# A selective-scan decoder layer: B and C in one transfer per scan group

## The reference, cut to what matters

```python
dbc = jnp.einsum('bld,rd->blr', u, W_x)
dt_in = dbc[..., :DTR]                    # DTR = 16
Bm = dbc[..., DTR:DTR + DSTATE]           # DSTATE = 16
Cm = dbc[..., DTR + DSTATE:]
dA = jnp.exp(dt[..., None] * A)
dBu = dt[..., None] * Bm[:, :, None, :] * u[..., None]
def step(h, e):
    da, dbu, c = e
    h = da * h + dbu
    y = jnp.einsum('bdn,bn->bd', h, c)
    return (h, y)
```

## Time and profile before

| what | value |
|---|---|
| median of 3 runs | 1865.69 us (1863.43 to 1866.33) |
| the profiled execution | 1863.23 us, of which the span is 1861.2 us |
| busy: TensorE, VectorE, ScalarE, GpSimd | 73%, 73%, 53%, 48% |
| moved by DMA | 188.89 MB, mean 101 GB/s |
| mean granted clock of TensorE | 0.849 of full speed |

### The profile page before, as it was taken

The page is one execution under the profiler, slowest core; times in us unless marked ns, Lnnn a source line. Parts: engine busy times, 40 slices in busy tenths (PEclk is TensorE's granted clock), DMA queues, the critical chain, the costliest instruction groups (busy, mean ns, idle before and its releaser), DMA issues.

```text
span 1861.2 us, 16320 instructions
## 1 busy us (share of the span) xinstructions
PE 1366.2 (73%) x5472; PEld 826.3 (44%) x5472; DVE 1350.9 (73%) x1509; ACT 987.5 (53%) x1519; POOL 898.0 (48%) x459
## 2 busy tenths in 40 slices
PE   5555767686797758885778667887588857786975
PEld 2344344453455335552456334553355434562433
DVE  3987588957876888867888687867878778773142
ACT  4432665547663655647554655637465566534532
POOL 0665077615764266624666165642667155651110
PEclk9555978897899879998799978998799978998988
DMA  5632343205330532206321343305332153310000
GB/s 182 241 124 79 100 163 118 86 26 214 113 109 27 189 108 102 80 24 204 113 101 56 120 136 114 106 23 183 102 112 79 36 193 112 112 34 0 12 0 23
DMA packets 64762, 188.89 MB, mean 101 GB/s; under 512 B 6224, under 2 KB 22480, under 8 KB 64720
## 3 DMA queue, kind: packets, MB, share of 16 engines
q1 hardware_dynamic: 64720, 188.37, 29.3%
HBM read 183.62 MB, written 4.72 MB: 101 GB/s over the span
## 4 chain that ended last, share of the span: by engine, by line
PE 40%; DVE 31%; ACT 15%; issue 6%; POOL 5%; DMA 2%; ACTq 0%; DVEq 0%; POOLq 0%; SPq 0%; another core or an unknown queue 0%
DVE reg_a L1078 16%; DVE pb L1069 8%; PE py L645 6%; PE pc L631 5%; PE pc L623 4%; PE pb L486 4%; PE pb L605 3%; POOL reg_a L443 3%; ACT reg_a L875 2%; PE px L549 2%; PE px L527 2%; DMA x_out<-reg_m 2%; PE pb L587 2%; ACT xs L778 2%; DVE reg_m L927 1%
## 5 line engine op out<-in xcount | busy, mean ns | idle before, releaser
L443 POOL TENSOR_TENSOR reg_a<-reg_a,cb 128x1024 f32<-128x1024 f32 x256 | 611.7, 2391 | 438.1 <-DVE reg_a L1078 437.8
L1078 DVE TENSOR_TENSOR_SCAN reg_a<-reg_a,pb 128x1024 f32<-128x1024 f32 x256 | 584.6, 2283 | 143.5 <-ACT reg_a L875 110.2
L875 ACT ACTIVATE reg_a<-dt,neg_a 128x511 f32<-128x511 f32 x512 | 335.6, 711 | 165.3 <-DVE reg_a L1078 164.6
L645 PE MATMUL py<-ident,reg_a 128*128 128x128 f32 x2048 | 329.9, 318 | 70.6 <-POOL reg_a L443 70.6
L645 PEld LDWEIGHTS py<-ident,reg_a 128*128 128x128 f32 x2048 | 288.9, 167 | 167.6 <-POOL reg_a L443 104.9
L1069 DVE TENSOR_TENSOR pb<-bb,pb 128x1024 f32<-128x1024 f32 x256 | 314.6, 1229 | 29.7 <-ACT reg_y L835 2.6
L564 PE MATMUL pb<-ex,vw 64*128 64x512 f32 x48 | 46.9, 1075 | 146.9 <-DVE px L994 146.9
L623 PE MATMUL pc<-x2T,w_fc 128*128 128x512 f32 x224 | 119.0, 658 | 28.1 <-DVE reg_y L1095 21.2
L549 PE MATMUL px<-hT,whh 128*128 128x512 f32 x288 | 137.4, 613 | 0.4 <-ACT xs L778 0.4
L631 PE MATMUL pc<-w_pr,reg_m 128*128 128x256 f32 x448 | 109.8, 396 | 7.0 <-ACT y_sb L798 4.1
L405 POOL TENSOR_TENSOR xs<-xs,hT 128x1024 f32<-128x1024 f32 x24 | 56.6, 2358 | 96.2 <-ACT xs L786 96.2
(11 more groups left out here) (174 smaller groups left out, 2259.5 us busy)
## 6 DMA issues: line engine op xcount, KB each, us to landing
bb<-bc_rows SPq DMA_DIRECT2D x256, 512.0 KB, 3.7
cb<-bc_rows SPq DMA_DIRECT2D x64, 512.0 KB, 6.0
xin<-x_in SPq DMA_DIRECT2D x9, 512.0 KB, 3.6
xs<-x_in SPq DMA_DIRECT2D x8, 512.0 KB, 3.6
x_out<-reg_m SPq DMA_DIRECT2D x8, 512.0 KB, 3.4
w_in<-w_inT_in SPq DMA_DIRECT2D x1, 1024.0 KB, 7.1
w_fc<-w_fcT_in SPq DMA_DIRECT2D x1, 1024.0 KB, 10.9
w_pr<-w_prT_in SPq DMA_DIRECT2D x1, 1024.0 KB, 13.1
```

The lines of the kernel that those rows point to most:

```text
L443: pool.tensor_tensor(h[:, g % HR], h[:, g % HR], cb[:, 2 * q:2 * q + 2], ALU.mult).then_inc(s["hc_done"], 1)
L645: mm = pe.matmul(py[:, cols_], h[:, g % HR, j, cols_], ident[:], is_transpose=True, start=(q == 0 and j == 0 and i2 == 0), stop=(q == PAIR ...
L875: ins = act.activation(d_a[:, g % 2, j, 1:], dt[:, c, 1:], ACT.Exp, scale=neg_a[:, c * NS + n + j:c * NS + n + j + 1])
L1078: dve.tensor_tensor_scan(h2[:, g % HR], d_a2[:, g % 2], pb[:, 1:3, :].rearrange("p a t -> p (a t)"), 0.0, ALU.mult, ALU.add).then_inc(s["s ...
```

## The change

B and C of a group come in one transfer of 1 MB. `bc` is a ring of four slots, each with two rows of B and two rows of C. `cb` is gone, so C is loaded again for every chunk: 32 transfers of 1 MB in an iteration in place of 32 + 8 of 512 KB. So that the four rows of a pair lie side by side in DRAM, the columns of `w_x` are put in the order B, B, C, C on the host, and the set-up scales the columns of B in eight pieces. A slot is free again when GpSimd's product with C is done (`hc_done`), not when `mul` is.

```diff
-HB = 3
+HB = 4
...
-        cb = sb("cb", [P, NS, L])
         xp = sb("xp", [P, L])
-        bb = sb("bb", [P, HB, 2, L])
+        bc = sb("bc", [P, HB, 4, L])
...
-        def pair(half, q):
-
-            return bc_dram[half, 2 * q:2 * q + 2, :].rearrange("n t -> (n t)").partition_broadcast(P)
+        def pair(q):
+
+            return bc_dram[4 * q:4 * q + 4, :].rearrange("n t -> (n t)").partition_broadcast(P)
...
                     for half in range(2):
-                        sp_.dma_start(bc_dram[half], xp[Q * half + DTR:Q * (half + 1), :]).then_inc(s["bc_out"], 16)
+                        sp_.dma_start(bc_dram[NS * half:NS * (half + 1), :], xp[Q * half + DTR:Q * (half + 1), :]).then_inc(s["bc_out"], 16)
                     sp_.wait_ge(s["bc_out"], 32)
                     for g in range(GROUPS):
                         q = g % PAIRS
                         if g >= HB:
-                            sp_.wait_ge(s["mul_done"], g - HB + 1)
-                        sp_.dma_start(bb[:, g % HB].rearrange("p n t -> p (n t)"), pair(0, q)).then_inc(s[f"b_in{g % HB}"], 16)
+                            sp_.wait_ge(s["hc_done"], g - HB + 1)
+                        sp_.dma_start(bc[:, g % HB].rearrange("p n t -> p (n t)"), pair(q)).then_inc(s[f"bc_in{g % HB}"], 16)
                         if g == STORE_AT and spikes:
                             store_out(i)
-                        if g < PAIRS:
-                            sp_.dma_start(cb[:, 2 * q:2 * q + 2, :].rearrange("p n t -> p (n t)"), pair(1, q)).then_inc(s[f"cb_in{q}"], 16)
...
                         pool.wait_ge(s["scan_done"], g + 1)
-                        pool.wait_ge(s[f"cb_in{q}"], 16)
-                        pool.tensor_tensor(h[:, g % HR], h[:, g % HR], cb[:, 2 * q:2 * q + 2], ALU.mult).then_inc(s["hc_done"], 1)
+                        pool.wait_ge(s[f"bc_in{g % HB}"], 16 * (g // HB + 1))
+                        pool.tensor_tensor(h[:, g % HR], h[:, g % HR], bc[:, g % HB, 2:4], ALU.mult).then_inc(s["hc_done"], 1)
...
-            dve.tensor_scalar(w_x[:, :, DTR:Q], w_x[:, :, DTR:Q], 0.5, None, ALU.mult)
+            for half in range(2):
+                for q in range(PAIRS // 2):
+                    b_cols = w_x[:, :, Q * half + DTR + 4 * q:Q * half + DTR + 4 * q + 2]
+                    dve.tensor_scalar(b_cols, b_cols, 0.5, None, ALU.mult)
...
-                    dve.wait_ge(s[f"b_in{g % HB}"], 16 * (g // HB + 1))
+                    dve.wait_ge(s[f"bc_in{g % HB}"], 16 * (g // HB + 1))
...
-                    dve.tensor_tensor(pb[:, 1:3, :], bb[:, g % HB], pb[:, 0:1, :].to_broadcast([P, 2, L]),
+                    dve.tensor_tensor(pb[:, 1:3, :], bc[:, g % HB, 0:2], pb[:, 0:1, :].to_broadcast([P, 2, L]),
                                       ALU.mult).then_inc(s["mul_done"], 1)
```

More of the change, by code:

```diff
@@ L85 @@
 z_full zth_ready sz_ready sp_abs sp_exp sp_ln dt_ready dtu_ready da_zero yt_ready yback_full
-bc_kept bc_out cb_in0 cb_in1 cb_in2 cb_in3 cb_in4 cb_in5 cb_in6 cb_in7 b_in0 b_in1 b_in2 da_ready mul_done scan_done hc_done hsum_done ypost_done yz_done
+bc_kept bc_out bc_in0 bc_in1 bc_in2 bc_in3 da_ready mul_done scan_done hc_done hsum_done ypost_done yz_done
 op_half op_full res_done post_stat post_aggr post_ve post_rs post_norm post_full hT_loaded
@@ L1129 @@
     w_x = w["L0_attn_W_x"].T
+    w_bc = w_x[:, DTR:].reshape(DIN, 2, PAIRS, 2).transpose(0, 2, 1, 3).reshape(DIN, BC)
     blank = np.zeros((DIN, Q - DTR), w_x.dtype)
@@ L1137 @@
         "w_inT_in": w["L0_attn_W_in"].T,
-        "w_xT_in": np.concatenate([w_x[:, :DTR], w_x[:, DTR:DTR + NS], w_x[:, :DTR], w_x[:, DTR + NS:],
+        "w_xT_in": np.concatenate([w_x[:, :DTR], w_bc[:, :NS], w_x[:, :DTR], w_bc[:, NS:],
                                    w_x[:, :DTR], blank, w_x[:, :DTR], blank], axis=1),
@@ L1148 @@
     out = nc.dram_tensor("x_out", (BATCH, L, E), F32, kind="ExternalOutput").ap()
-    bc_dram = nc.dram_tensor("bc_rows", (2, NS, L), F32, kind="Internal").ap()
+    bc_dram = nc.dram_tensor("bc_rows", (BC, L), F32, kind="Internal").ap()
     decoder_layer(nc, bc_dram, *args, out)
```

## The result

The changed kernel takes 1878.68 us in the median (1878.44 to 1882.86, 4 runs), against 1864.74 us (1863.43 to 1866.33, 4 runs) for the one before: 1.008 of it, 95% interval [1.0062, 1.0097]. It is 13.9 us slower. The forecast was no change, 1867.2 us.

The account below looks back on a forecast made before the run. TensorE and VectorE bound the kernel, loads being off the path; 1.5 us lost at one head and 0 elsewhere, on the 1865.69 us median, gave 1867.2 us, called no change, range 1861 to 1874.

Parts of the forecast that it names:

- What it adds: Extra loads, later slot release, set-up scalings: seven more cost under 7 x 0.75 = 5 us uncovered, nothing under 11.19 us idle.
- Can the transfers carry it: Densest stretch of groups: 1 MB per 3.7 us needs 283 GB/s; DMA had moved 399 GB/s, so groups would not stretch.
- How late 1 MB lands: Loads into `bc`: complete 5.0 to 5.7 us after issue in the ring, 6.6 us at a batch's head.
- Head of batch 0: First load lands after 6.6 us; scan 2.4 us later, 1.0 us hidden by ScalarE's decay: 1.5 us lost.
- Heads of 1 to 7: First load may land 8.3 us after issue because the scan waits for the decay; 6.6 us fits, nothing lost.
- The ring: Four slots: from product g-4's end to `mul` g at least 7.2 us, median 11.8; landing 5.7 us, so nothing lost.
- The skill's figure: Landing of 1 MB by the skill page: 6.15 us transfer plus about 2.0 fixed, near 8.2; sum 5.6 instead of 1.5 us.
- the slow transfer: Rival: 1 MB transfers slow in themselves, costing in the ring and heads; 1869.3 to 1887.2 us, chance 0.12.
- the slow heads: Rival: at batch heads four queued 1 MB transfers delay the first beyond 8.3 us; 11.2 us, 1876.9 us, chance 0.05.
- the slower engines: Rival: doubled traffic slows `mul` and scan by 1% in 192 groups; 6.7 us, 1872.4 us, chance 0.03.
- It becomes faster: Rival: engine interlocking shifts TensorE work between clock levels, up to 8 us either way; chance 0.05 faster, 0.05 slower.
- a sign of being wrong: The forecast is wrong if `mul` waits for loads in many groups or TensorE's clock by windows differs from before.

Follow-up runs that it names:

- e8: The kernel before, its one scaling of the B columns cut into four pieces and 128 tiny VectorE instructions added in the set-up (131 more): 1878.05 us, ratio 1.0077.
- e2: The kernel before, its one scaling of the B columns cut into eight (seven VectorE instructions more), without the new loads: 1877.65 us, ratio 1.0077.
- e1: The changed kernel with its eight scalings of the B columns made one strided instruction: 1864.82 us, ratio 1.0002 to the kernel before.
- e5: The changed kernel with one strided scaling instruction and a ring of three slots in place of four: 1876.59 us, ratio 1.0070 to the kernel before.
- e3: The kernel before, its one scaling of the B columns cut into four (three VectorE instructions more): 1877.67 us, ratio 1.0069.
- e9: The kernel before with three tiny VectorE instructions at the end of the hardware loop's body, none more ahead of it: 1877.69 us, ratio 1.0067.

## Why the prediction was wrong

**The step that failed** is in "What it adds", the set-up: seven more small scalings were to cost less than 5 us without the cover of 11.19 us of idle time, and "with it nothing". As work they did cost nothing. VectorE stood idle for 11.38 us behind them after the change too. In e8 131 tiny ones, 8.01 us, left it 4.22 us. But an instruction has a second cost, its place in the program. The prediction priced each added instruction by its duration and never asked what it moves. That term was put at 0 and is 12.4 to 13.9 us (e2, and the change itself). In its place the runs showed the reload of code at each of the four turns: 17.1 us, of which 3.2 us came back later in the iterations. For the rest of the change the forecast of no change held (e1, ratio 1.0002).

The sum, from the profiles: 17.1 us at the four turns, 3.2 us gained back in the loop's iterations (0.7 to 0.9 us each in batches 4 to 7), and 1.3 us that the first three batches ended later, together 15.2 us, as the span is longer (1876.4 against 1861.2). The 1.3 us is not a loss of the change: e1's loop too begins 1.3 us later than before in its profile (624.60 against 623.35), at the same median. Where the 0.7 to 0.9 us come from stays open.

**Can the transfers carry it:** right. Windows of batch 0 after; the last three columns are TensorE's clock, the DMA share and GB/s:

```profile
47.00:53.00 6.00, 0.00 (x0) 0.00 (x0) 4.97 (x4) 4.86 (x9) 1.59 (x1) 0.50 1.00 422
...
60.00:100.00 40.00, 25.98 (x108) 19.89 (x108) 34.63 (x23) 14.26 (x23) 28.29 (x14) 0.63 0.73 271
```

271 GB/s at a share of 0.73, with 283 forecast for the densest pace. The backlog moved at 422 GB/s where the half transfers made 399.

**How late 1 MB lands:** mis-sized, on the safe side. 4.7 us in the median where I took 5.0 to 5.7, and 4.5 us for the first load at the head of batch 0 where I took 6.6. A pair of transfers was a poor stand-in: one transfer is complete sooner than two with half the bytes each. The first of four queued was not held up by the three behind it (4.3 to 4.9 us at the eight heads).

**Head of batch 0:** forecast 1.5 us lost, measured 0.0. `mul(0)` started 4.5 us after the issue and not 6.6, all of it under the decay. **Heads of 1 to 7:** right; first scan 9.62 to 9.64 us after the issue in both kernels.

**The ring:** right. No `mul` and no product waited for a load there. But the margin was thinner than the 5.7 us of landing made it. In e1 four loads in a row in batch 1 landed 7.3 to 8.0 us after their issue. GpSimd's catching up had released the first three 2.3 us apart, and a 16 KB code transfer on queue 8 began beside the first. The first of them was in time by 0.3 us. What slowed them was not separated. With three slots 23 waits appear (e5).

**The skill's figure.** The Trainium skill, "DMA: Bandwidth & Descriptors", gave an estimate of 8.2 us by its table and fixed cost. Both are stated there for transfers that GpSimd issues, and SyncE issues these. No run agrees: a load of 1 MB lands after 4.6 to 4.7 us in the median (e1, the changed kernel). Its formula in the section "Anatomy of one DMA", 2.0 us and the bytes at 436 GB/s, is 4.4 us as an estimate, and that is near.

**The rivals:** the slow transfer, the slow heads and the slower engines all fell (`mul` 1230 ns). "It becomes faster" named the interlocking of engines and TensorE's clock as what could move the time either way; the granted clock is 0.845 after and 0.849 before. By windows it does differ at the turns (0.65 where it was 1.00), which the prediction gave as a sign of being wrong. That is worth some 0.55 us a turn, 2.2 us in all, and comes behind the stall; it is not its cause, as e2 has both without the traffic. The right rival, that the program's code has to be fetched too, was not among them. It could have been: the page shows queues of instructions in part 3, and the kernel has one hardware loop.

## What to carry to other kernels

When an edit adds or removes instructions ahead of a hardware loop or in it, price them twice: their time, and what they do to the number of code blocks that the loop body touches on that engine. A loss of the same size at every turn of the loop, "issue" as the releaser of its first instructions, and more records of the instruction queue are the signs of it. A padding of a few instructions, or one strided instruction for eight, tells it from the change's own work, and it should be tried before a change is judged: here the same 101 MB of added traffic is "0.8% slower" or "no change" by seven tiny instructions.

## What the runs showed of the hardware

- VectorE's code came in 8 KB transfers on queue 14. A loop body of 264 instructions ran for five iterations with none of them in one position, and with five an iteration in another. A repeat after 128 instructions fits the times (3 and 131 slow; 0, 1, 10 and 23 fast) and the transfers ahead of the loop (124 to 130 records apart). In the changed kernel the cost was about 4.3 us a turn, less 0.8 us later in the iteration; in e3, e8 and e9 a turn grew by 3.2 to 4.0 us.
- The Trainium skill, "Runtime: NRT & Kernel Launch", section "Instruction fetch mechanics", says that a taken branch to code outside the fetched window makes the engine wait for a transfer. The trace agrees (the branch at 1039.93, the next instruction at 1042.76). The page gives blocks of 16 KB, 256 instructions; the transfers here are of 8 KB, and e3 and e8 speak for 128. Why three blocks stay and four do not was not measured.
- One broadcast load of 1 MB landed after 4.7 us in the median, one of 512 KB after 3.7 us, so the second half megabyte costs 1.0 us.
- A late start of one engine can cost more on another. Behind VectorE's stall TensorE's granted clock fell to its lower level (1.2 GHz) for part of a stretch where it had been at the higher one (2.4 GHz), and eight matmuls took 4.24 us in place of 2.79.
